# A fused attention and expert kernel: new order at the hand-over, TensorE repeats, larger root groups, and scatters that wait for an earlier landing

## The reference, cut to what matters

```python
# x: 16 batches x 512 positions x 128 channels, 16 heads of 8
q, k, v, gate = (x @ W.T for W in (Wq, Wk, Wv, Wg)); beta = sigmoid(x @ Wb.T)
alpha = exp(-exp(A_log) * softplus(x @ Wa.T + dt_bias)); q, k = normalised by head
def step(S, (k_t, q_t, v_t, beta_t, a_t)):          # over the 512 positions
    S = S * a_t
    S = S + k_t * ((v_t - k_t . S) * beta_t)
    return S, q_t . S
x = layernorm(x + (rmsnorm(ys) * silu(gate)) @ Wo.T + bo)
expert = argmax(x @ router_w.T)                     # one of 8 experts for each token
y = (silu(x @ gate_w[expert].T) * (x @ up_w[expert].T)) @ down_w[expert].T   # inner width 352
out = layernorm(x + y)
```

## Time and profile before

| | us |
|---|---|
| median of 3 runs | 781.5 (775.88 to 783.81) |
| profiled execution, its own time | 779.52 |
| its span, first to last instruction | 777.7 |
| PE, DVE, ACT, POOL busy | 677.5, 610.1, 415.8, 654.0 |
| mean granted TensorE clock | 0.928 of full speed |

### The profile page before, as it was taken

One profiled execution on the slowest core, in us unless ns is written; L12 is line 12 of the kernel. 1 busy time (PEld: TensorE's weight loads), 2 busy tenths in 40 slices (PEclk: granted clock), 3 DMA queues, 4 the chain that ended last, 5 costly groups with the idle time before them and its releaser, 6 DMA issues.

```text
span 777.7 us, 13705 instructions
## 1 busy us (share of the span) xinstructions
PE 677.5 (87%) x3545; PEld 507.4 (65%) x3545; DVE 610.1 (78%) x1554; ACT 415.8 (53%) x1281; POOL 654.0 (84%) x800
## 2 busy tenths in 40 slices
PE   8779798989989899999989989697788879999990
PEld 3446374756657575565756657575667879999990
DVE  3899999999999999999999999999953523333340
ACT  6735456564565656466565555433314346666660
POOL 2899899999999999999999999999755756766664
PEclk9889899999999999999999999799869999999995
DMA  6733233443333334333234232206346456777720
GB/s 175 198 97 98 69 98 86 114 116 90 86 90 94 89 112 116 96 85 102 82 105 120 77 97 71 85 22 220 136 164 184 166 182 226 240 237 235 238 97 9
DMA packets 135917, 97.27 MB, mean 125 GB/s; under 512 B 95630, under 2 KB 110225, under 8 KB 135714
## 3 DMA queue, kind: packets, MB, share of 16 engines
q1 hardware_dynamic: 130514, 87.55, 38.2%
q0 software_dynamic: 4320, 8.43, 3.4%
q10 hardware_dynamic: 1008, 0.43, 0.2%
HBM read 39.80 MB, written 31.43 MB: 92 GB/s over the span
## 4 chain that ended last, share of the span: by engine, by line
DVE 35%; PE 29%; POOL 20%; issue 5%; ACT 5%; DMA 3%; SPq 2%; POOLq 0%; DVEq 0%; ACTq 0%
PE banks L432 11%; DVE banks L1817 6%; DVE upd L1805 6%; POOL q_prod L1255 6%; PE banks L654 5%; PE banks L445 5%; DVE banks L1791 5%; DVE prod L1775 4%; DVE banks L1801 4%; DVE mix L1795 3%; POOL u L1255 3%; DVE upd L1786 3%; POOL solve L1255 2%; POOL kkqk L1255 2%; POOL u_tmp L1255 1%
## 5 line engine op out<-in xcount | busy, mean ns | idle before, releaser
L1255 POOL TENSOR_TENSOR q_prod<-s_keep,q_gam 128x512 f32<-128x512 f32 x128 | 139.9, 1097 | 12.0 <-ACT s_keep L965 11.7
L707 PE MATMUL banks<-q_prod,ident 128*128 128x256 f32 x496 | 118.9, 395 | 21.6 <-POOL q_prod L1255 21.4
L965 ACT ACTIVATE s_keep<-banks 128x128 f32<-128x128 f32 x128 | 49.8, 389 | 156.7 <-DVE upd L1805 156.6
L707 PEld LDWEIGHTS banks<-q_prod,ident 128*128 128x128 f32 x496 | 95.7, 198 | 46.2 <-POOL q_prod L1255 32.4
L542 DVE TENSOR_TENSOR hid<-banks,silu 128x384 f32<-128x384 f32 x71 | 39.6, 557 | 96.4 <-PE banks L432 83.8
L432 PE MATMUL banks<-xs_t,w_tile 128*128 128x128 f32 x852 | 108.9, 278 | 3.5 <-ACT silu L473 3.5
L1817 DVE TENSOR_REDUCE banks<-upd 128x128 f32<-128x640 f32 x127 | 105.0, 827 | 7.6 <-ACT z_s L1194 0.5
L432 PEld LDWEIGHTS banks<-xs_t,w_tile 128*128 128x128 f32 x852 | 102.4, 194 | 4.4 <-issue 4.3
L1791 DVE TENSOR_REDUCE banks<-prod 128x64 f32<-128x576 f32 x128 | 93.7, 732 | 0.0
L654 PE MATMUL banks<-kkqk,ident 128*128 128x320 f32 (+2 forms) x272 | 84.5, 471 | 7.7 <-ACT y_rms L993 4.3
L1775 DVE TENSOR_TENSOR prod<-banks,k_gam 128x512 f32<-128x512 f32 x128 | 88.1, 688 | 2.9
(11 more groups left out here) (214 smaller groups left out, 1442.3 us busy)
## 6 DMA issues: line engine op xcount, KB each, us to landing
w_tile<-gate_up_we SPq DMA_DIRECT2D x71, 352.0 KB, 3.0
xs<-x_sorted SPq DMA_DIRECT2D x71, 64.5 KB, 2.4
x_ct<-in_x_ct SPq DMA_DIRECT2D x16, 256.0 KB, 3.2
k_dram<-kq_s SPq DMA_DIRECT2D x16, 256.0 KB, 2.9
q_dram<-kq_s SPq DMA_DIRECT2D x16, 256.0 KB, 3.6
out<-v_s SPq DMA_DIRECT2D x16, 256.0 KB, 2.7
out<-beta SPq DMA_DIRECT2D x16, 256.0 KB, 2.6
k_h<-k_dram SPq DMA_DIRECT2D x16, 256.0 KB, 3.0
```

What stands on the lines that cost most here:

```text
L707: i = mm(out, ident[:, :], q_prod[m][:, :, d, :], start=(m == 0 and d == 0), stop=(d == DH - 1), skip_group_check=True)
L1255: b.step(label, win, lambda: tt(out, x, y, op))
```

## The change

Seven windows instead of six open the first part, so TA is 21. In the last window GpSimd sends 15 tiles instead of 13, in other portions between the products. Every indirect DMA of either kind waits for the landing of the last but one of its kind. TensorE gets four batches of repeated 128x512 products whose result nobody reads (22 in all), and the router product, the last query sums, the counts and the projection stand at other places of its order. ScalarE copies the last state before it copies the turned tile. SP fills the regions and loads rows earlier, beside the weights. The root groups are longer at first, rows are scaled from `step` TA+1 on at 7 rows in 5 steps, and the last three root groups are computed on ScalarE as logarithm and exponential, after one load of its table. TensorE's order in the tail behind the norm sums was: experts -3, -2, residual, -1, 0, attention, 1, count, 2, turn, 3, count, router, 4, 5, count. It becomes: experts -3, -2, residual, -1, count, 0, count, 1, attention, 2, 3, 4, turn, 5, router, 6, count. VectorE makes the second table behind the expert step instead of ahead of it. The diff, cut:

```diff
-WA = 6
+WA = 7
...
-        PE_TAIL, ACT_TAIL, DVE_TAIL = 6, 4, 6
+        PE_TAIL, ACT_TAIL, DVE_TAIL = 7, 6, 8
...
         def to_sorted(eng, t0, t1):
             for m in range(t0, t1):
+                part, n = (s_sorted_a, m) if m < WA * TW else (s_sorted, m - WA * TW)
+                if n >= 2:
+                    eng.wait_ge(part[n % 2], 16 * (n // 2))
...
         def finish_sync(eng):
-            fill_regions(eng)
-            for tile in range(TA, TA + NG - 1):
+            for tile in range(TA, TA + 4):
                 load_weights(eng, tile)
-            eng.wait_ge(s_sorted, 16 * (NT - WA * TW))
+            for n in range(2):
+                eng.wait_ge(s_sorted[n], 16 * len(range(n, NT - WA * TW, 2)))
             eng.wait_ge(s_pad, 16 * (1 + E))
             for tile in range(TA, TA + NG):
                 load_rows(eng, tile)
+            load_weights(eng, TA + NG - 2)
...
-        roots = [0] + list(range(TA - 4, NF - 3, 3)) + [NF - 2, NF - 1, NF]
+        roots = [0, TA - 4, TA + 6, TA + 14, TA + 21, TA + 27] + list(range(TA + 31, NF - 3, 3))
+        ROOTS_POOL = len(roots) - 1
+        roots += [NF - 2, NF - 1, NF]
+        NORM = TA + 1
...
-            done = max(n for n in range(len(roots)) if roots[n] <= max(step - 2, TA - 4)) if step < NF + 3 else -1
-            return min(roots[done], 8 + (4 * (step - (TA - 3)) + 2) // 3)
+            done = max(n for n in range(len(roots)) if roots[n] <= (step if n > ROOTS_POOL else step - 2))
+            return min(roots[done], 8 + (7 * (step - NORM) + 2) // 5)
...
+            def last_root(n):
+                first, last = roots[n], roots[n + 1]
+                after(eng, s_var, last - 1)
+                nc.scalar.activation(rstd2[:, first:last], var2[:, first:last], ACT.Ln).then_inc(s_log, 1)
+                after(eng, s_log, n - ROOTS_POOL)
+                nc.scalar.activation(rstd2[:, first:last], rstd2[:, first:last], ACT.Exp, scale=-0.5).then_inc(s_rstd_last, 1)
...
+                if step == NF - 3:
+                    nc.scalar.preload_act_table_set("natural_log_exp_and_others")
...
             def scatter(tile):
                 after(eng, s_norm, tile)
+                after_scatter(eng, tile - 2)
...
-            for n in range(len(roots) - 1):
+            for n in range(ROOTS_POOL):
...
-                until = min(a if n else 4, 4 * (n + 1))
+                until = b - 3 if n > 5 else b - 5
...
+            def keep_busy(n, times):
+                def go():
+                    for _ in range(times):
+                        i = mm(y_ps[0], ident[:, :], w_proj[:, 0:4, :], start=True, stop=True, skip_group_check=True)
+                    return i
+                b.step(f"warm{n}", w, go)
...
                 y_chunks(w, 0)
+                b.wait(dve, "y_n7", p)
+                keep_busy(0, 8)
                 attention(p)
                 late_chunks("y1", 4, 6)
-                late_chunks("y1_6", 6, 7)
+                keep_busy(1, 4)
                 turn(p)
-                router(p)
+                keep_busy(2, 8)
                 return
             if b.tail:
-                late_chunks("y1_7", 7, 8)
                 b.wait(dve, "y_prod3", p)
-                y_deltas()
+                y_deltas("y_near")
+                late_chunks("y", 6, 8)
+                router(o)
+                keep_busy(3, 2)
                 y_sums(p, post_ps[:, 0:2 * T])
...
                 keep(NCH * w + 6)
+                keep(NCH * w + 7)
                 x1_turned(p)
-                keep(NCH * w + 7)
-                router_logits(p)
...
-                sort_to(w0 + 4, w0 + 6)
+                sort_to(w0 + 4, w0 + 7)
                 q_times_s(w, 3)
-                sort_to(w0 + 6, w0 + 8)
+                sort_to(w0 + 7, w0 + 10)
                 q_times_s(w, 4)
-                sort_to(w0 + 8, w0 + 10)
+                sort_to(w0 + 10, w0 + 12)
                 context(p)
                 q_times_s(w, 5)
-                sort_to(w0 + 10, w0 + 12)
+                sort_to(w0 + 12, w0 + 15)
                 q_times_s(w, 6)
-                sort_to(w0 + 12, w0 + 13)
...
                 sort_to(w0, w0 + 10)
                 context(p)
-                sort_to(w0 + 10, w0 + 14)
+                sort_to(w0 + 10, w0 + 13)
...
                 y_store()
-                load_rows(e, NG)
-                load_rows(e, NG + 1)
                 y_load()
-                for tile in range(NG + 2, TA):
-                    load_rows(e, tile)
-                for tile in range(NG, TA):
+                for tile in range(4, 17):
                     load_weights(e, tile)
+                    load_rows(e, tile + 1)
+                fill_regions(e)
+                for tile in range(17, TA):
+                    load_weights(e, tile)
+                    if tile + 1 < TA:
+                        load_rows(e, tile + 1)
```

More of the change, by code:

```diff
@@ L207, in block_kernel @@
         s_table_a, s_table_b, s_fill, s_pad = sem("s_table_a"), sem("s_table_b"), sem("s_fill"), sem("s_pad")
-        s_sorted_a, s_sorted = sem("s_sorted_a"), sem("s_sorted")
+        s_sorted_a, s_sorted = ([sem(f"s_sorted_{part}{n}") for n in range(2)] for part in "ab")
         s_xs, s_scat = [sem(f"s_xs{n}") for n in range(NR)], [sem(f"s_scat{n}") for n in range(NO)]
@@ L462, in expert_act, with squares @@
                 A(xs_t[tile % NX][:, :], turn_ps(tile)[:, 0:P], ACT.Copy).then_inc(s_xt, 1)
[L463 to L468, removed]
+            def squares():
+                tile = step - 1
+                if 0 <= tile < NF:
+                    after(eng, s_sum, tile)
+                    after(eng, s_var, tile - 2)
+                    A(res2_sq[tile % 2][:, :], res2[tile % NV][:, :], ACT.Square, scale=D ** -0.5,
+                      accum_out=var2[:, tile:tile + 1]).then_inc(s_var, 1)
+            if step >= TA:
+                squares()
             tile = step + 2
@@ L497, in finish_act @@
                 expert_act(eng, step)
-                if step > TA - 3:
+                if step == NF - 3:
+                    nc.scalar.preload_act_table_set("natural_log_exp_and_others")
+                for n in range(ROOTS_POOL, len(roots) - 1):
+                    if step == roots[n + 1]:
+                        last_root(n)
+                if step > NORM:
                     for tile in range(normed(step - 1), normed(step)):
                         norm(tile)
-            assert normed(NF + 3) == NF
+            assert normed(NF) == NF
         def finish_pool(eng):
@@ L875, in pe_body @@
                 count(NW - 2)
+                if not b.dry:
+                    expert_pe(b.eng, 1)
+                attention(p)
+                if not b.dry:
+                    expert_pe(b.eng, 2)
+                    expert_pe(b.eng, 3)
+                    expert_pe(b.eng, 4)
+                turn(p)
+                if not b.dry:
+                    expert_pe(b.eng, 5)
                 router(p)
                 if not b.dry:
[L878 to L879 removed]
+                    expert_pe(b.eng, 6)
                 b.wait(dve, "before", NW - 2)
@@ L1167, in act_body @@
                     nc.scalar.preload_act_table_set("silu_and_others")
-                    for step in range(-3, 1):
+                    for step in range(-3, 2):
                         expert_act(b.eng, step)
@@ L1727, in last_outputs @@
                 if not b.dry:
-                    for k in range(n_table_a, n_steps_a):
-                        table_a(e, k)
+                    down_means(e)
                     centre_down(e)
@@ L1738, in last_outputs @@
                 if not b.dry:
-                    for step in range(-2, 2):
+                    for k in range(n_table_a, n_steps_a):
+                        table_a(e, k)
+                    for step in range(-2, 0):
                         expert_dve(e, step)
@@ L1745, in last_outputs @@
                 if not b.dry:
-                    for step in range(2, 4):
+                    for step in range(2):
                         expert_dve(e, step)
@@ L1750, in last_outputs @@
                 if not b.dry:
-                    expert_dve(e, 4)
+                    for step in range(2, 5):
+                        expert_dve(e, step)
+                    expert_dve(e, 5)
                 for k in range(5):
@@ L1754, in last_outputs @@
                 if not b.dry:
-                    expert_dve(e, 5)
-                for k in range(5, 10):
+                    expert_dve(e, 6)
+                for k in range(5, 7):
                     route_part(NW - 1, k)
+                b.wait(dve, "ends", NW - 1)
+                if not b.dry:
+                    table_b(e, 0, 5)
+                    expert_dve(e, 7)
+                for k in range(7, 10):
+                    route_part(NW - 1, k)
+                b.wait(dve, "place", NW - 1)
+                if not b.dry:
+                    table_b(e, 5, 7)
             def chunk(c):
```

62 lines of the change are left out of this document (33 added, 29 removed).

## The result

The changed kernel takes **815.0 us** (median of 4 runs, 808.8 to 816.8) against 781.2 before in the same job: a ratio of 1.042, 95% interval 1.036 to 1.049. The forecast was 785, with 767 to 797 as its range. The profiled execution took 808.8, its span is 806.9, its mean granted clock 0.929.

A forecast was written before the change was run, and what follows sets the result against it. It took TensorE to bound the long expert stretch before the change, and GpSimd to end last after it. Terms summed to +3.3 us: 779.5 becomes 782.8, by the median 781.5 becomes 785; range 767 to 797 for 8 in 10.

The forecast's parts named there:

- distance of two indirect DMAs under the wait: Sorting and output: a landing of 2.7 plus a start of 0.3, halved, gives 1.5 us instead of the natural 1.27.
- The output: GpSimd's 71 scatters at 1.5 us, ten roots 12 us: last landing 129.4 us after the first rows, 772.9 against 769.6.
- rival 1: Sorting and output: the wait is hardly ever the last one, distance 1.3, -9.6 us, 772 us; chance 0.25.
- The sorting: Behind the attention's root: 22 distances of 1.5 us, last issue 638.4, first rows 643.5, 5.6 us later than before.
- The wait in the last window: The third sorted tile, issued at 543.35 before, waits for a landing until 546.5, 3.1 us late.
- The repeats: TensorE's last window: repeats cost 18.7 us, the clock gives back some 6; norm sums end at 588.3, 5.2 us late.
- The late scaling of rows: ScalarE scales rows four steps later: the first scatter starts 10.2 us after the first rows, formerly issued before they came.
- The last roots on ScalarE: Three roots leave GpSimd's last stretch, where they cost 1.6 us more than the usual gap; the table load costs nothing.
- The second table: VectorE's table behind the expert step takes away three short TensorE waits, some 3 us, all inside the hole.
- The drain: End of the kernel: 7.9 us after the last landing in which the trace shows no work, kept unchanged.
- rival 3: End of the kernel: the drain shrinks with at most two indirect DMAs open, by up to 7.9 us, about 765; chance 0.06.
- Rival 2: Sorting and output: landings as in the sorting rows, distance 1.65 in both stretches, +17 us, 798 us; chance 0.15.

The follow-up runs named there:

- x1: The changed kernel without either landing wait, in sorting or output; all else stays: 774.5 us, ratio 0.990.
- x8: The changed kernel with each indirect DMA waiting for the landing of the last but three of its kind instead of the last but one: 774.6 us, ratio 0.990.
- y1: The changed kernel without both landing waits and without the 22 repeats, x7 once more in another job: 767.7 us, ratio 0.982.
- y5: y1 with SP loading rows 18 to 20 before filling regions, two weight loads instead of four ahead of the first rows, and 7 repeats: 763.0 us, ratio 0.980.
- x2: The changed kernel with the landing wait taken out of the sorting DMAs alone: 798.8 us, ratio 1.022.
- x4: The changed kernel with each scatter's two waits exchanged, landing first and scaled rows second: 799.7 us, ratio 1.021.
- x3: The changed kernel with the landing wait taken out of the output scatters alone: 790.8 us, ratio 1.009.
- x7: The changed kernel without both landing waits and without the 22 repeats: 767.5 us, ratio 0.979.
- x5: The kernel before with both landing waits added and nothing else of the change: 792.9 us, ratio 1.014.
- y2: y1 with the root groups, the row scaling schedule and the roots on GpSimd as they were before: 771.9 us, ratio 0.986.
- x6: The changed kernel, landing waits kept, without the 22 repeated products of TensorE: 800.3 us, ratio 1.024.
- y4: y1 with 7 of the 22 repeats, three ahead of the projection and four ahead of the delta sums: 765.7 us, ratio 0.981.
- x11: The changed kernel without waits or repeats, with SP's rows 18 to 20 earlier and fewer weight loads first, on a slower chip: 836.1 us, ratio 1.018.

## Why the prediction was wrong

**The bounds it read** were right: GpSimd ends last, ScalarE waits for roots, TensorE waits for ScalarE, the hole stays. The step that failed is the price of the new wait: the **distance of two indirect DMAs under the wait**, put at 1.5 in both stretches. It was 1.81 in the sorting and 1.70 in the output.

*Of the 26.1 us* that the span ends later than predicted, the table at the top gives: 3.4 that were there at the first tile of the last window already (the profiles of x1 to x8 and y1 to y5 have that tile between 539.9 and 543.4, without regard to their waits or repeats, so I take them to be one execution's difference from another; in the kernels with the repeats the norm sums follow this tile to within 0.4 us, 46.3 after it in x1 and x2 and 46.7 in x8); 2.0 up to the first sorted tile behind the root; 6.8 for 22 sorting distances; -0.7 for the load of the rows; 0.1 to the first scatter; 14.5 for the output. The forecast also put the profiled execution 2.0 under the median, and it was 6.1.

*The output, 14.5.* The prediction took "2.7 and 0.3, halved". The landing was nearly right: 2.8. The 0.3 was read from DMAs that had waited for nothing or for an engine. Behind a landing, with two waits at one DMA and the landing's written last, it is 0.75, and x4 shows that this 0.45 is real by taking it away: of the 0.2 that a distance is too long, 0.13 go with it, 8.8 us in all. The other 0.08, some 5.5 us, stay in x4 (1.58) and are not taken apart by a run. The likely cause is that a long landing costs its whole length and a short one gives nothing back, which the prediction named under rival 1 and then did not put into its number. Halving a pair is itself only a rough price: (2.8 + 0.75) / 2 would be 1.78, more than the 1.70 measured, since by the table of waits a landing ends the wait of 24 scatters only, and a scaled row that of 13. At the quiet end 1.5 was right by accident, 2.2 and 0.75.

*The sorting, 6.8.* Here the start behind a landing is 0.27 in most links of the chain and 0.75 in one of those shown (637.08 to 637.84); that DMA is the first of a portion of the sorting, for which GpSimd also waits for VectorE's places, so it has two waits like a scatter, with the landing's written last. With 0.3 to 0.4 on average, 1.81 means landings of 3.2 to 3.3, over the 3.1 that the prediction held as its upper bound. For these DMAs as a whole the changed kernel's trace gives no landing, so that is worked out. But x3 and x4 sort with the same wait, and there they can be read (issue to landing of the sorting behind the root, x3 and then x4):

```profile
DMA to landing us min/median/max: 2.3/3.3/6.1
...
DMA to landing us min/median/max: 2.3/3.4/5.1
```

The nearest row was not the scatters but the sorting landings themselves.

*The wait in the last window* was right in kind and close in size: a landing of 6.4, the third tile 7.1 us behind the first where 3.6 was natural, so 3.5 late for the 3.1 predicted. The 0.4 is again the start of a DMA with two waits.

*The repeats* were taken as +5.2 together with that wait, and their end was forecast well: 588.3, and x1, which has no wait, 586.2. But it was set against the wrong neighbour. The new order alone ends at 578.6 (x7), not at 583.1: it gains 4.5, the repeats cost 7.7, and the two hid each other in one number. In the time of the kernel that is 7 without and 9 to 15 with the waits. The prediction let the clock give back some 6 us. Between x7 and x1 it is about 3: the stretch from the query sums to the norm sums takes 34.4 in x1, with 19.0 of repeats, and 26.0 in x7, with 7.3 of waits. Part of the clock came with the new order alone, 0.83 instead of 0.59.

*The late scaling of rows* was counted, with its 10.2 us (10.3 measured), but not what it may do to the wait: the waits add 4.5 us to the output stretch in the old order (x5) and 22.5 in the new one (against x1). The late scaling is the likely reason, as said at x5.

*The last roots on ScalarE* were held for 1.6; together with the larger groups they are worth 4.2, in y1 against y2. *The second table* behind the expert step was not tried by itself, nor were the seventh window and the new orders of TensorE and SP; together, with all that y2 keeps of the change, they are worth 10 us (771.9 against 782.2). *The drain*: the span ends 8.0 us after the last landing in the changed kernel and 7.9 in x1, so rival 3 is out. *Rival 1* asked for 772 if the wait were never last; x1, which has no wait, and x8, where it is hardly ever last, gave 774.5 and 774.6. Its mechanism was not the case, its price was right. Its estimate from the Trainium skill (DMA: Bandwidth & Descriptors, Anatomy of one DMA — SWDGE path), 2.15 us, again agrees with the quiet end alone: 2.1 to 2.2 there, a median of 2.8 under load. *Rival 2*, 798 us, was the nearest and was given 0.15. It was right for the sorting, where landings were as long as the sorting rows showed or longer. In the output its 1.65 came near for another reason: landings there were 2.8, and the start was 0.75. The chances named for the range of 767 to 797 add up to 0.74, not to 8 in 10.

The kernel's medians taken apart, over several jobs: 771.9 for the new order (y2), -4.2 for the roots (y1), +6.8 for the repeats (x1), +24.3 and +16.3 for the two waits: 815. The two waits are nearly all of what makes the change a loss.

## What to carry to other kernels

A wait that throttles a queue of DMAs sets a distance of up to (landing + start behind the landing) / depth; here that gave 1.78 where 1.70 was measured. Take the mean landing under the load of that very stretch, not the median of a calmer one, and the start from a DMA that really waited for a landing. Waiting for the last but three instead of the last but one cost nothing here, and four natural distances (5.1 us) are longer than nearly all landings. Price two edits of one stretch separately even when they are made together, since a gain and a loss hide in their sum; and ask of each edit what slack it removes from another.

## What was not expected of the hardware

- With two waits at one indirect DMA, the one written last became an instruction of its own, and a landing waited for there started the DMA after 0.75 us instead of 0.3 (changed kernel and x4). Two lines exchanged brought 8.8 us between the first and the last of 71 scatters.
- Without the landing waits the repeats lifted the granted clock at 560 to 580 us from 0.83 to 1.00 (x7 and x1) and still cost 7 us; beside the landing waits it was 0.91 there with the repeats (changed kernel) and without them (x6), and over 540 to 600 us 0.94 and 0.83. Seven repeats where TensorE waited anyway gave 0.97 and a kernel 2.0 us faster (y4 against y1), which is within the noise of the two; the norm sums start 1.9 earlier in the trace.
- On one chip the kernel before took 819.6 us instead of 780 to 783, and in x11, profiled there, TensorE waited up to 8 us in the hand-over without a named cause; there the kernels that are 2% faster elsewhere were 1.3 to 1.8% slower.
- The end of the span lay 8.1, 8.0 and 7.9 us behind the last landing in the kernel before, the changed one and x1 (for the first and the last with a landing of 2.2 taken from the rows near it), though GpSimd's drain itself took 11.2, 10.1 and 14.2 us: the longer drain begins earlier and ends with the same delay.
